# A fused two-layer network on one core: a new rule and new ranks for the constant products and the order of attention, and the first product of the second expert list in three rounded parts

## The reference

```python
# layer 0, first half: attention, 16 query heads of 8, 4 key heads
xn = x * rsqrt(mean(x * x) + EPS) * norm_w
q, k, v = xn @ w_q, xn @ w_k, xn @ w_v           # q and k times a rotary factor
p = softmax(where(causal, q k' / sqrt(8), -inf))
x + (p v) @ w_o
# layer 0, second half: 8 experts of 128 -> 512 -> 128 with gelu, each token
# goes to 2 of them with its weights; one shared expert for all tokens
# layer 1, first half: gated recurrence along the tokens, then a gated
# product pair 128 -> 512 -> 128 with silu
# layer 1, second half: token mixing, relu squared, sigmoid gate
```

## Time and profile before

| What | Value |
|---|---|
| Median of three runs | 836.71 us |
| The profiled execution | 837.36 us |
| Its span, first to last instruction | 835.6 us |
| Mean granted TensorE clock | 0.940 |
| PE busy | 776.5 us (93%) |
| DVE, ACT, POOL busy | 483.3, 494.4, 360.8 us |
| L1046 (up products of tiles) | 312 records of 383 ns |
| L1057 (down products of tiles) | 624 records of 275 ns |
| L920 (score maxima products) | 192 records of 521 ns |

### The profile page before, as it was taken

The page is one execution under the profiler, slowest core; times in us unless marked ns, Lnnn a source line. Parts: engine busy times, 40 slices in busy tenths (PEclk is TensorE's granted clock), DMA queues, the critical chain, the costliest instruction groups (busy, mean ns, idle before and its releaser), DMA issues.

```text
span 835.6 us, 12440 instructions
## 1 busy us (share of the span) xinstructions
PE 776.5 (93%) x3706; PEld 466.9 (56%) x3706; DVE 483.3 (58%) x1862; ACT 494.4 (59%) x744; POOL 360.8 (43%) x540
## 2 busy tenths in 40 slices
PE   5889999999899998998899999999999999999994
PEld 4443444364454643554699889997666544444442
DVE  4396778587478786965424422220345687857473
ACT  1756666565837665554644545554478768888563
POOL 6425344444635666736142411113444465613073
PEclk9988999789879898798899999999999999999998
DMA  9990000000000000001767576641100000000003
GB/s 282 382 342 1 1 1 0 1 5 20 4 16 11 20 20 20 20 2 32 222 208 204 169 212 206 212 133 35 33 29 26 20 25 26 26 6 1 0 13 89
DMA packets 59712, 64.18 MB, mean 77 GB/s; under 512 B 6331, under 2 KB 42525, under 8 KB 59645
## 3 DMA queue, kind: packets, MB, share of 16 engines
q1 hardware_dynamic: 53266, 49.84, 19.2%
q0 software_dynamic: 6320, 13.53, 5.1%
q10 hardware_dynamic: 58, 0.02, 0.0%
HBM read 35.18 MB, written 28.18 MB: 76 GB/s over the span
## 4 chain that ended last, share of the span: by engine, by line
PE 64%; DVE 11%; POOL 6%; issue 5%; ACT 3%; DMA 2%; POOLq 0%; DVEq 0%; ACTq 0%
PE PS L1057 10%; PE PS L1046 8%; DVE JK L1249 4%; PE PS L920 4%; PE PS L958 4%; PE PS L1113 2%; PE PS L1120 2%; PE PS L875 2%; PE PS L1043 2%; PE PS L943 2%; PE PS L1127 2%; PE PS L869 2%; PE PS L863 2%; PE PS L960 2%; PE PS L929 2%
## 5 line engine op out<-in xcount | busy, mean ns | idle before, releaser
L1249 DVE CUSTOM_DVE_ANT_0 JK<-PS,CM 128x256 bf16<-128x256 f32 (+1 forms) x512 | 147.8, 351 | 30.5 <-PE PS L920 29.6
L1729 ACT ACTIVATE GF<-PS,XN 128x256 f32<-128x256 f32 x156 | 73.5, 473 | 77.0 <-PE PS L1046 74.5
L920 PE MATMUL PS<-KZ,QS 128*128 128x512 f32 x192 | 91.1, 521 | 6.9 <-DVE MX L1249 5.1
L1057 PEld LDWEIGHTS PS<-WD,GF 128*128 128x128 f32 x624 | 91.2, 191 | 8.8 <-ACT GF L1729 1.3
L1057 PE MATMUL PS<-WD,GF 128*128 128x128 f32 x624 | 94.9, 275 | 1.0 <-ACT GF L1729 0.6
L1046 PE MATMUL PS<-XS,WU 128*128 128x256 f32 x312 | 93.2, 383 | 1.7 <-DVE XS L1473 1.0
L1879 POOL DMA_INDIRECT expert_rows<-five,IU x64 | 64.1, 1001 | 59.8 <-DVE IU L1354 32.0
L1901 POOL DMA_INDIRECT got<-expert_out,IG x64 | 64.0, 1000 | 51.4 <-DMA got<-expert_out,IG 35.2
L1829 POOL TENSOR_SCALAR H<-xc,MOD 128x256 f32<-128x256 f32 x56 | 33.7, 610 | 115.7 <-DVE xc L1218 115.1
L1683 ACT ACTIVATE PA<-PS 128x1024 f32<-128x1024 f32 x64 | 64.4, 1022 | 21.7 <-PE PS L943 21.5
L1866 POOL TENSOR_SCALAR_AFFINE_SELECT PA<-PA 128x256 f32<-128x256 f32 x128 | 49.0, 410 | 57.1 <-ACT PA L1683 55.6
(11 more groups left out here) (285 smaller groups left out, 1614.0 us busy)
## 6 DMA issues: line engine op xcount, KB each, us to landing
expert_rows<-five SPq DMA_DIRECT2D x16, 1024.0 KB, 13.4
WU<-in_L_ffn_up_w SPq DMA_DIRECT2D x39, 256.0 KB, 2.7
WD<-in_L_ffn_down_w SPq DMA_DIRECT2D x39, 256.0 KB, 3.1
XT<-expert_rows SPq DMA_DIRECT2D x39, 128.0 KB, 3.2
expert_out<-YT POOLq DMA_DIRECT2D x39, 128.0 KB
PA<-in_L_attn_x SPq DMA_DIRECT2D x8, 256.0 KB, 5.4
out<-yo SPq DMA_DIRECT2D x8, 256.0 KB, 2.3
expert_rows<-five,IU POOLq DMA_INDIRECT x64
```

The costliest lines, as they stand in the source:

```text
L920: pe.matmul(bk.rearrange("p (j n) -> p j n", n=wd), q, ks, start=True, stop=True).then_inc(sems["mx_mm"], 1)
L1057: m = pe.matmul(bk[:, b], g[:, b], wd[:, k, :], start=(k == 0 and t == 0), stop=(k == 3 and t == TB - 1 and kind == "t"))
L1249: m = dve.tensor_tensor_reduce(JK[n % 2][:, s], bk[:, s], CM[:, 256 - wd:256] if wd == 128 else CM[:, 0:256], -1.0, 3.0e38, ALU.add, ALU.m ...
L1729: act.activation(GF[slot["gf", kind, u, k]][:, 0:n], bank("up", kind, u, k)[:, 0:n], ACT.Gelu, bias=bias).then_inc(sems["gelu"], 1)
```

## The change

There are three parts.

The constant products. `arrange` keeps a list `busy` of the intervals in which TensorE works in the plan; `atm`, `mxm` and `spm` count there with less than their slot (`ACTIVE`). `fill` looks back over WINDOW of plan time before the stage at hand. If the work in it is under LEAST = 0.6 of it, constant products go in the gap before the stage, up to its end less SPARE. Then, if it is still under WORST = 0.5, and the stage takes a bank of a ring itself, up to MOST = 2 constant products are put down in that bank ahead of the stage, and the stage is planned later by their time. The same rule serves both plans.

The ranks `FIRST` are other numbers, and GRAIN goes from 0.3 to 0.2. `FIRST2` and GRAIN2 stay.

The second list. Per tile, VectorE rounds WU into WH (`wsh`), GpSimd subtracts it from WU into WO (`wsl`), and `xs` makes XH, the rounded rows, and XL, the rest. `up` then has three products of rounded operands in one bank in place of one fp32 product. The product of the two rests is not computed. The first list stays as it is. `wsh` and `wsl` of tile t + 1 are put down after block 0 of tile t, and `xt` and `xs` of it after block 1, where these stood after block 2. Both new stages stand in `FIRST`, and neither is among the planner's jobs.

```diff
 FIRST = {
-    **dict.fromkeys(("mh", "qmt", "qma",), 17.0),
-    **dict.fromkeys(("plan_tiles", "plan_bias", "plan_rows",), -9.0),
+    **dict.fromkeys(("mh", "qmt", "qma",), 42.0),
+    **dict.fromkeys(("plan_tiles", "plan_bias", "plan_rows", "kzp", "kza",), 4.0),
     **dict.fromkeys(("spm", "spe",), 8.0),
-    **dict.fromkeys(("kzp", "kza",), -1.0),
-    **dict.fromkeys(("fetch", "xt", "xs",), 5.0),
-    **dict.fromkeys(("nrt", "nrd",), 53.0),
-    **dict.fromkeys(("gelu",), -15.0),
+    **dict.fromkeys(("fetch", "xt", "xs",), 16.0),
     **dict.fromkeys(("lc", "ln_sq", "ln_var", "ln_rs", "ln_norm", "ln_mod",), 7.0),
-    **dict.fromkeys(("pv", "ot",), 62.0),
-    **dict.fromkeys(("dpm", "dpd",), -4.0),
-    **dict.fromkeys(("tw",), -13.0),
-    **dict.fromkeys(("atm", "ate", "causal",), -16.0),
-    **dict.fromkeys(("scatter",), -11.0)
+    **dict.fromkeys(("dpm", "dpd", "scatter",), 2.0),
+    **dict.fromkeys(("tw",), -61.0),
+    **dict.fromkeys(("atm", "ate", "causal",), -1.0),
+    **dict.fromkeys(("wsh", "wsl",), -47.0),
+    **dict.fromkeys(("stt", "sta", "wom", "woh",), 6.0)
 }
-IDLE, FILLED, ONE = 1.0, 0.75, 0.215
+WINDOW, LEAST, WORST, MOST, ONE, SPARE = 3.4, 0.6, 0.5, 2, 0.215, 0.1
...
+ACTIVE = {"atm": 0.12, "mxm": 0.23, "spm": 0.46}
-HOP, SWITCH, GRAIN = 0.08, 1.3, 0.3
+HOP, SWITCH, GRAIN = 0.08, 1.3, 0.2
...
+def fill(P, banks, done, busy, since, until, own):
+    def lack(share):
+        return share * WINDOW - sum(max(0.0, b - max(a, until - WINDOW)) for a, b in busy[-60:])
+
+    def put(ring, k, to, size, begin):
+        n = P.count.get("fill", 0)
+        P.slot[("fill", n)], P.prior[("fill", n)] = to, ring.ends.get(k, ())
+        P.put("fill", n, size)
+        busy.append((begin, begin + size * ONE))
+
+    room = [(max(since, when), number(k), ring, k) for ring, number in banks for k, when in [ring.free(done)] if k is not None]
+    if room:
+        begin, to, ring, k = min(room, key=lambda x: x[:2])
+        size = int(min(lack(LEAST), until - begin - SPARE) / ONE)
+        if size > 0:
+            put(ring, k, to, size, begin)
     for ring, number in banks:
+        if ring in own and until > 20.0:
+            size = min(MOST, int(lack(WORST) / ONE))
+            if size > 0:
+                k, _ = ring.free(done)
+                put(ring, k, number(k), size, until)
+                until += size * ONE
+            break
+    return until
...
         if engine == "PE":
-            fill(P, banks, done, free.get("PE", 0.0), end - held)
+            end = fill(P, banks, done, busy, free.get("PE", 0.0), end - held, [ring for ring, *_ in takes]) + held
+            busy.append((end - held, end - held + ACTIVE.get(stage, held)))
...
+    def weights_in(t):
+        take(WS2, "ws", t, end=("up", "t", t, 3))
+        put("wsh", t)
+        put("wsl", t)
+
+    weights_in(N1)
     rows_in(N1)
...
-            if k == 2 and t + 1 < NT:
+            if k == 0 and t + 1 < NT:
+                weights_in(t + 1)
+            if k == 1 and t + 1 < NT:
                 rows_in(t + 1)
...
+                w.wait_ge(*at("w_hi", u))
+                w.wait_ge(*at("w_lo", u))
+                xh, xl = (a[slot["xs", u]][:, :] for a in (XH, XL))
+                wh, wo_ = (a[slot["ws", u]][:, f] for a in (WH, WO))
+                pe.matmul(bk[:, 0:TR], wh, xh, start=True, stop=False)
+                pe.matmul(bk[:, 0:TR], wo_, xh, start=False, stop=False)
+                pe.matmul(bk[:, 0:TR], wh, xl, start=False, stop=True).then_inc(sems["up"], 1)
...
+            n = own(dve.tensor_copy(h[:, :], a))
+            w.wait_ge(*n)
+            dve.tensor_tensor(XL[slot["xs", t]][:, :], a, h[:, :].bitcast(F), ALU.subtract).then_inc(sems["xs"], 1)
+
+        def wsh(t):
+            w.wait_ge(*at(*att_done))
+            w.wait_ge(ld_t[t % NF], 48 * (t // NF + 1))
+            for e in prior["ws", t]:
+                w.wait_ge(*at(*e))
+            dve.tensor_copy(WH[slot["ws", t]][:, :], WU[t % NF][:, :]).then_inc(sems["w_hi"], 1)
...
+        def wsl(t):
+            w.wait_ge(ld_t[t % NF], 48 * (t // NF + 1))
+            w.wait_ge(*at("w_hi", t))
+            pool.tensor_tensor(WO[slot["ws", t]][:, :], WU[t % NF][:, :], WH[slot["ws", t]][:, :].bitcast(F), ALU.subtract
+                               ).then_inc(sems["w_lo"], 1)
```

More of the change, by code:

```diff
@@ L88 @@
     "gelu": ("ACT", 0.58, "gelu"), "t_up": ("PE", 0.43, None), "t_gelu": ("ACT", 0.4, "gelu"), "t_down": ("PE", 0.43, None),
-    "t_ev": ("DVE", 0.36, None), "xt": ("PE", 0.22, None), "xs": ("DVE", 0.36, None), "store_rows": ("POOL", 0.55, None),
+    "t_ev": ("DVE", 0.36, None), "xt": ("PE", 0.22, None), "xs": ("DVE", 0.36, None), "wsh": ("DVE", 0.5, None), "wsl": ("POOL", 1.22, None), "store_rows": ("POOL", 0.55, None),
     "gather": ("POOL", 2.4, None), "cmb": ("DVE", 2.25, None), "fin1": ("DVE", 1.95, None), "fin2": ("PE", 0.5, None),
@@ L200, in tails @@
     return tail
-def fill(P, banks, done, since, until):
-    for ring, number in banks:
[L206 to L211, removed]
+def fill(P, banks, done, busy, since, until, own):
[12 more added lines that the diff above has]
+            put(ring, k, to, size, begin)
+    for ring, number in banks:
+        if ring in own and until > 20.0:
[6 more added lines that the diff above has]
+    return until
 def arrange(P, jobs, done, grain, first, banks=(), more={}):
@@ L220, in arrange @@
     tail = tails(jobs, more)
+    busy = []
     for x in tail:
@@ L279 @@
     "pl_ei": "plan_tiles", "pl_ub": "plan_bias", "pl_ix": "plan_rows", "pl_w": "plan_rows",
-    "rw_tp": "rows", "rw": "rows", "xt_tp": "xt", "xs": "xs", "up": "up", "gelu": "gelu", "down": "down", "ev": "ev",
+    "rw_tp": "rows", "rw": "rows", "xt_tp": "xt", "xs": "xs", "w_hi": "wsh", "w_lo": "wsl", "up": "up", "gelu": "gelu", "down": "down", "ev": "ev",
     "cmb": "cmb", "fin": "fin1", "fin_bk": "fin2", "moe_x": "fin3", "cen": "lc",
@@ L297, in schedule @@
     LT, LH, LL, LN = (Ring(range(2)) for _ in range(4))
-    GF, WTS, XS = Ring(range(6)), Ring(range(2)), Ring(range(2))
+    GF, WTS, XS, WS2 = Ring(range(6)), Ring(range(2)), Ring(range(2)), Ring(range(2))
     def stage(name, *key, takes=(), after=()):
@@ L732, in program @@
     XS = [sb(f"XS{k}", [128, TR], where=moe) for k in range(2)]
+    XH, XL = ([sb(f"{n}{k}", [128, TR], R, where=moe) for k in range(2)] for n in ("XH", "XL"))
+    WH, WO = ([sb(f"{n}{k}", [128, FF], R, where=moe) for k in range(2)] for n in ("WH", "WO"))
     YT = [sb(f"YT{k}", [128, TR], where=moe) for k in range(3)]
@@ L1045, in up @@
                 w.wait_ge(*at("xs", u))
-                pe.matmul(bk[:, 0:TR], WU[u % NF][:, f], XS[slot["xs", u]][:, :], start=True, stop=True).then_inc(sems["up"], 1)
+                if u < N1:
+                    pe.matmul(bk[:, 0:TR], WU[u % NF][:, f], XS[slot["xs", u]][:, :], start=True, stop=True).then_inc(sems["up"], 1)
+                    return
+                w.wait_ge(*at("w_hi", u))
[5 more added lines that the diff above has]
+                pe.matmul(bk[:, 0:TR], wh, xl, start=False, stop=True).then_inc(sems["up"], 1)
         def down(kind, u, k):
@@ L1472, in xs @@
                 w.wait_ge(*at(*e))
-            dve.tensor_copy(XS[slot["xs", t]][:, :], bank("xt", t)[:, 0:TR]).then_inc(sems["xs"], 1)
+            h, a = XH[slot["xs", t]], bank("xt", t)[:, 0:TR]
+            if t < N1:
+                dve.tensor_copy(XS[slot["xs", t]][:, :], a).then_inc(sems["xs"], 1)
+                return
+            n = own(dve.tensor_copy(h[:, :], a))
[7 more added lines that the diff above has]
+            dve.tensor_copy(WH[slot["ws", t]][:, :], WU[t % NF][:, :]).then_inc(sems["w_hi"], 1)
         def ev(kind, u):
@@ L1586, in vector @@
               "rtl": rtl, "rt_cmp": rt_cmp, "rt_tie": rt_tie, "rt_rank": rt_rank, "rt_sum": rt_sum,
-              "rt_out": rt_out, "dpd": dpd, "plan_tiles": plan_tiles, "plan_bias": plan_bias, "plan_rows": plan_rows, "xs": xs, "ev": ev,
+              "rt_out": rt_out, "dpd": dpd, "plan_tiles": plan_tiles, "plan_bias": plan_bias, "plan_rows": plan_rows, "xs": xs, "wsh": wsh, "ev": ev,
               "cmb": cmb, "fin1": fin1,
@@ L1926, in gpsimd @@
         zero = pool.to_reg(0.0)
-        do = {"ln_mod": ln_mod, "wq": wq, "pjl": pjl, "kzp": kzp, "causal": causal, "scatter": scatter, "store_rows": store_rows, "gather": gather,
+        do = {"ln_mod": ln_mod, "wq": wq, "pjl": pjl, "kzp": kzp, "causal": causal, "scatter": scatter, "wsl": wsl, "store_rows": store_rows, "gather": gather,
               "hy": hy, "mix0": mix0, "ux": ux}
```

## The result

The changed kernel takes 812.69 us in the median (805.13 to 815.81, four runs) against 835.9 for the kernel before (four runs). The ratio is 0.9715, interval 0.9635 to 0.9796: 23 us, 2.9% faster. The forecast was 822, with a range of 803 to 843.

What follows compares the result with a forecast made beforehand. TensorE was taken to set the time everywhere, through its clock in the first stage and its products in the second list. From 837.4 us, -4.4 and -10.5 gave 822.5, stated as a median of 822, range 803 to 843.

Steps and rivals of the forecast that it cites:

- The second list: Second list of expert tiles: three rounded products for one fp32 gain 6.2 us, the first tile costs 1.8; net -4.4 us.
- an up product at 0.37 us: Second list: three rounded products take 0.37 us per up product, midway between 0.33 and 0.41, instead of 0.44.
- loads laid bare: Second list: weight loads not overlapped, 0.65 us per up product, a loss of 18.5 us; rival at 847 us, chance 0.06.
- The first tile's charge of 1.8 us: Start of the second list: first up product waits for wsl behind a store on GpSimd; 1.8 us once, bounds 0 and 3.
- The deadlines of xs and wsl: Second list: both ready in time, xs covered by 1 us, wsl complete about 2.0 us into a tile of 3.4.
- The constant products: Attention and routing, 60 to 400 us: about 150 products win 18.5 us of half-clock time, cost 8; gain 10.5 us.
- the price of a quarter on the path: 60 to 400 us: a quarter of the constant products' 33 us delays TensorE, charged 8 us, bounds 0 and 33.
- The new ranks: Order up to about 410 us, with finer grain: changes only which engine waits; put at 0, bounds 21 us either way.
- Full success: First stage: clock at its full level throughout, constant products lying in TensorE's waits; 801 us, chance 0.15.
- The rival in which the products don't hold the clock: First stage: added constant products are hidden and the stage stays as long; 833 us, chance 0.22.
- The slower one, forced products on the path: First stage: 33 us of constant products lie on TensorE's path for 18.5 us regained; 847.5 us, chance 0.12.
- my list of signs: Expected traces: three records at 0.12 us, tiles of 3.4 to 3.5, clock 0.95 or more, some 300 constant-product records.

Runs made afterwards that it cites:

- after_silent: Changed kernel in its own order, its 55 planned constant products not issued: 815.35 us, ratio 0.9789 to the kernel before.
- no_list: Changed kernel with the second list put back as before; new ranks, grain and rule stay: 814.24 us, ratio 0.9758 to the kernel before.
- rule_only: Kernel before with only the new rule for constant products, 101 instead of 19, old ranks and grain: 841.94 us, ratio 1.0064.
- after_double: Changed kernel with each constant product issued twice as often, 110 instead of 55, same order: 812.62 us, ratio 0.9792 to the kernel before.
- rule_only_silent: Kernel before, old ranks planned under the new rule, the 101 constant products not issued: 860.47 us, ratio 1.0341.
- after_gaps_only: Changed kernel with no forced constant products (MOST = 0), those in gaps of the plan stay: 824.74 us, ratio 0.9858 to the kernel before.
- after_grain3: Changed kernel with GRAIN back at 0.3, everything else new, 84 constant products: 836.34 us, ratio 1.0038 to the kernel before.
- before_silent: Kernel before in its own order, its 19 constant products not issued: 839.27 us, ratio 0.9957.

## Why the prediction was right, and where it was wrong

The direction and the range were right, and the total by its own terms came out 8 us short: 14.9 us expected, 23 measured. That the range held is in good part luck: 10.5 of the 14.9 stood on the constant products, which by after_silent are worth between nothing and some 6 us here, and the larger part of the gain, about 13 us by the same run, came from the term put at 0. Point by point:

**What bounds the kernel.** Right: TensorE and its clock in stage 1, TensorE's products in the second list. The 21.6 us came from stage 1 and the two lists and none from layer 1.

**The second list.** Taken: -4.4 us. Against no_list it is 4.0 to 4.5, against the kernel before 3.4, each with the fall of the clock in it, and 4.9 in after_silent without the fall. Its terms: an up product at 0.37 us; measured (3.43 - 4 x 0.44 - 0.22) / 4 = 0.36, the products at 0.12 between the two near bounds of 0.11 and 0.137. The step from loads laid bare (0.22 each) did not occur, and with it the Trainium skill's sentence ("TensorE: Matmul & The Clock Gate", "What overlaps and what doesn't") disagrees with this case here too, since all three loads use all row groups. The first tile's charge of 1.8 us was right as a wait (3.35 - 1.56 = 1.8), by the chain foreseen on GpSimd. What was missed is the fall of the clock that can come behind it, 1.5 us where it came. The deadlines of xs and wsl held, as TensorE waited for neither after the start. The 0.69 charged to wsh was too high; a copy from SBUF to SBUF of 512 columns took 0.43.

**The constant products.** Taken: -18.5 for the clock, +8 for the price. The failed step is the sentence that gives the clock's gain to them. In the order of the changed kernel they are worth between nothing and some 6 us (after_silent), and in an order with old ranks the rule loses 5 (rule_only). The clock of 0.95 that the prediction named came, but without them it was 0.94. Their number was over-estimated: 33 between 60 and 400 us (66 records of L854), not 150. And the price of a quarter on the path is not seen: 55 more of them added nothing (after_double).

**The new ranks.** Taken: 0, with bounds of plus and minus 21 us. This is the term that was mis-sized. Alone they give 0.9861, and fitted to the rule they were planned with, 0.9758. I had written that an order changes only which engine waits; it did, and it also sets the clock, as the three ranges above show. Why it does (whether thin products come in a row less often) is argued and not shown. Which engine waits is seen in the groups of instructions. Kernel before, whole span, columns as in the earlier trace rows:

```profile
L1249 DVE CUSTOM_DVE_ANT_0 JK<-PS,CM 128x256 bf16<-128x256 f32 (+1 forms) x512 | 147.8, 351 | 30.5 <-PE PS L920 29.6
...
L1270 DVE TENSOR_TENSOR QM<-PS,QS 128x512 fp32r<-128x512 f32 x32 | 21.4, 688 | 23.0 <-PE PS L929 21.1 <-issue 1.7
```

and the changed kernel, the same two stages:

```profile
L1289 DVE CUSTOM_DVE_ANT_0 JK<-PS,CM 128x256 bf16<-128x256 f32 (+1 forms) x512 | 146.9, 352 | 20.6 <-PE PS L951 18.9
...
L1310 DVE TENSOR_TENSOR QM<-PS,QS 128x512 fp32r<-128x512 f32 x32 | 21.0, 684 | 7.6 <-PE PS L960 7.4
```

VectorE's work is the same to 1 us, and it waits 10 and 15 us less in front of these two. From 60 to 400 us it is busy in 258 us, not 247.

**The rivals.** Full success (801) did not occur: it wanted the full clock throughout the first stage, and 0.95 was measured. The rival in which the products don't hold the clock was wrong in general, since in rule_only they hold it well, and for the changed kernel's order it isn't decided, since there they hold little if anything. The slower one, forced products on the path, did not occur: rule_only_silent would have been faster than rule_only by it, and was about 20 us slower. What my list of signs said is mostly seen: three records at 0.12, tiles of 3.4 to 3.5 us, a clock of 0.95, no change behind 567 us; but about 300 records of the constant product were expected and 110 are there.

**What stays open.** Why this one order loses less of the clock is not settled. after_gaps_only and after_grain3 change nothing but the planner's numbers, and move the time by 12 and 27 us by the ratios, with clocks of 0.93 in the stage where after_silent has 0.94. So the clock explains only part of it; the rest is waits, and no run splits them from it. Nor was it tried to take a single rank back.

## What to carry to other kernels

Where a planner writes the order, a change to its ranks, its rounding or its account of time is a new order, and that can move the time by 2 to 3% with nothing added to the kernel's own work; charge it bounds from the waits of the stage, not zero. To learn what an added filler does, keep the order and leave the filler out (and issue it twice), as here: it was worth about 20 us in one order and too little to tell from zero in another. When a second unit prepares operands for a stage bound by TensorE, look at its first tile, where nothing hides the preparation; the gap was followed by a fall of the clock in some executions.

## What was not expected of the hardware

Two executions of one order differ by several us. The changed kernel and no_list are the same up to the last output product and came to it at 378.8 and 371.9. From the first output product (79.9 and 74.3) to the last they take 298.9 and 297.6, so attention isn't where these two part. They part in the first 25 us. The same twelve small products, in no_list and in the changed kernel:

```profile
13.74 1.41 PE L866 MATMUL PS<-scT,PA 128*128 128x16 f32 x12
```

```profile
13.80 2.58 PE L869 MATMUL PS<-scT,PA 128*128 128x16 f32 x12
```

A product that starts at 19.53 in no_list (L875) starts at 25.04 in the changed kernel (L878): 5.5 of the 6.9 us. The row of the changed kernel for this stretch shows no low clock, though the products go at about half the pace:

```profile
10.00:25.00 15.00, 14.98 (x51) 11.30 (x51) 3.66 (x24) 1.79 (x3) 5.80 (x15) 1.00 1.08 349
```

So in these 15 us the pace has to be read from durations.

The old order parts elsewhere: from the first score-maxima product to the last, before takes 323.4 us and before_silent 312.0, at 0.87 and 0.92 of the clock. (The first has its few constant products in it, the second has none.) Over all its sets of runs the kernel before ranged from 824.5 to 843.8 us. A comparison of 3 us therefore needs stages read from the traces rather than medians.

A wait in front of the second list's first product (TensorE busy for 0.39 of the 2.10 us from 469.4 to 471.5) was followed by a mean clock of 0.64 over the next 4.5 us. Three other traces with the same waits have 1.00 there, two with a wait of 2.5 us in one piece have 0.62. The same instructions can thus meet either clock, and a single trace doesn't tell which part of a loss is the gap's.
